# Weighted sums of two pairs together in slots 0 and 2 of an attention quad

## The reference

```python
attn = jnp.einsum('wqhd,wkhd->whqk', q * scale, k)
attn = attn + rel_bias[None]
attn = attn.reshape(B, nW, NH, N, N) + attn_mask[None, :, None]
attn = jax.nn.softmax(attn.reshape(B * nW, NH, N, N), axis=-1)
o = jnp.einsum('whqk,wkhd->wqhd', attn, v).reshape(B * nW, N, C)
o = o @ proj_w + proj_b
```

## Time and profile before

| | |
|---|---|
| median of 3 runs | 8522.53 us (8521.94 to 8527.99) |
| profiled execution | 8519.52 us, span of its instructions 8517.4 us |
| PE matmul busy | 7998.7 us, 94% of the span |
| PE weight loads | 5982.3 us, 70% |
| DVE, ACT, POOL busy | 72%, 60%, 63% |
| mean granted TensorE clock | 0.995 of full speed |

### The profile page before, as it was taken

One profiled execution on the slowest core, in us unless ns is written; L12 is line 12 of the kernel. 1 busy time (PEld: TensorE's weight loads), 2 busy tenths in 40 slices (PEclk: granted clock), 3 DMA queues, 4 the chain that ended last, 5 costly groups with the idle time before them and its releaser, 6 DMA issues.

```text
span 8517.4 us, 316110 instructions
## 1 busy us (share of the span) xinstructions
PE 7998.7 (94%) x111420; PEld 5982.3 (70%) x111420; DVE 6092.7 (72%) x18216; ACT 5147.7 (60%) x9120; POOL 5399.7 (63%) x6723
## 2 busy tenths in 40 slices
PE   3999999999999999999999999999999999999997
PEld 1777777777777777777767777777776677777766
DVE  4777767767776776776777677776686767777666
ACT  1755747646674664755767476574576647567456
POOL 6865646556785665655778465564677756556566
PEclk9999999999999999999999999999999999999998
DMA  2100010000011011000001101000100110000001
GB/s 42 22 13 10 15 27 15 10 12 13 10 21 31 13 20 22 15 6 16 9 15 21 27 16 27 15 15 4 20 4 19 24 22 15 7 13 14 6 19 23
DMA packets 596906, 142.14 MB, mean 17 GB/s; under 512 B 595660, under 2 KB 596256, under 8 KB 596471
## 3 DMA queue, kind: packets, MB, share of 16 engines
q1 hardware_dynamic: 574102, 131.41, 7.8%
q10 hardware_dynamic: 16865, 3.97, 0.3%
q0 software_dynamic: 5504, 1.21, 0.1%
HBM read 31.68 MB, written 19.27 MB: 6 GB/s over the span
## 4 chain that ended last, share of the span: by engine, by line
PE 71%; DVE 10%; issue 9%; ACT 3%; DVEq 2%; POOL 2%; ACTq 1%; POOLq 0%; DMA 0%
PE ps L876 12%; PE ps L932 11%; PE ps L838 8%; PE ps L864 7%; PE ps L948 7%; PE ps L977 7%; PE ps L883 5%; PE ps L901 4%; PE ps L911 3%; ACT PT L743 3%; DVE bst L995 2%; PE ps L819 2%; PE ps L920 2%; DVE xn L1114 2%; PE ps L962 2%
## 5 line engine op out<-in xcount | busy, mean ns | idle before, releaser
L618 POOL TENSOR_TENSOR S<-S,mx 113x588 f32<-113x588 f32 (+1 forms) x2048 | 2065.4, 1009 | 1543.8 <-DVE mx L1156 1539.4
L743 ACT ACTIVATE PT<-ps 98x588 f32<-98x588 f32 (+1 forms) x2048 | 1182.5, 577 | 1218.6 <-PE ps L932 1211.3
L1154 DVE TENSOR_TENSOR S<-ps,bias 113x588 f32<-113x588 f32 (+1 forms) x1536 | 963.4, 627 | 863.7 <-PE ps L864 863.7
L876 PEld LDWEIGHTS ps<-Vbd,PT 98*49 98x49 f32 x40960 | 1107.5, 125 | 658.6 <-issue 634.7
L876 PE MATMUL ps<-Vbd,PT 98*49 98x18 f32 (+1 forms) x40960 | 1321.4, 201 | 165.8 <-ACT PT L743 125.9
L1156 DVE TENSOR_REDUCE mx<-S 113x12 f32<-113x588 f32 (+1 forms) x2048 | 1359.6, 664 | 70.6
L932 PEld LDWEIGHTS ps<-ident,S 113*98 113x98 f32 x10240 | 1033.9, 128 | 477.6 <-issue 388.9
L932 PE MATMUL ps<-ident,S 113*98 113x113 f32 x10240 | 1338.7, 261 | 7.8 <-ACT S L725 4.6
L725 ACT ACTIVATE S<-S 113x588 f32<-113x588 f32 (+1 forms) x2048 | 1239.9, 605 | 63.1 <-POOL S L618 61.3
L948 PEld LDWEIGHTS ps<-w,G 128*98 128x98 f32 x12288 | 1149.8, 167 | 160.2 <-issue 86.3
L948 PE MATMUL ps<-w,G 128*98 128x96 f32 (+1 forms) x12288 | 1151.5, 250 | 2.7 <-DVE x L1221 2.4
(11 more groups left out here) (104 smaller groups left out, 10891.0 us busy)
## 6 DMA issues: line engine op xcount, KB each, us to landing
Vbd<-Vd SPq DMA_DIRECT2D x1536, 41.3 KB
Vbd<-Vd SPq DMA_DIRECT2D x512, 38.3 KB
mask<-L_conv_mask_matrix_dram SPq DMA_DIRECT2D x256, 37.5 KB
x<-x_dram SPq DMA_DIRECT2D x48, 84.0 KB
out_dram<-x SPq DMA_DIRECT2D x48, 84.0 KB
x<-x_dram SPq DMA_DIRECT2D x228, 10.5 KB
out_dram<-x SPq DMA_DIRECT2D x228, 10.5 KB
out_dram<-x SPq DMA_DIRECT2D x180, 18.4 KB
```

The costliest lines, as they stand in the source:

```text
L618: pool.tensor_tensor(v, v, m, ALU.subtract).then_inc(a_sub, 1)
L743: act.activation(PT[:, (s + 3) % 4, 0:blocks, :, :].rearrange("p (b t) w n -> p b (t w) n", b=banks), PTps[:, PT_BANK[l] - 3:PT_BANK[l] - ...
L876: last = pe.matmul(Ops[ROW2 * w:ROW2 * w + N, p, b, :].rearrange("p (a n) -> p a n", a=2), PT[:, p, b, w, :], v, start=True, stop=True)
L1154: dve.tensor_tensor(dst, scores, b, ALU.add).then_inc(a_bi, 1)
```

## The change

In PE's `attend` the weighted sums no longer stand in every slot. Slot 0 makes those of pairs 0 and 1 of quad i - 1, slot 2 those of pairs 2 and 3. The wait for a_o (now of quad i - 2) and for the spread of v stands at slot 0. Pairs 0 and 2 are thus summed one slot later than before (from slot 3 to slot 0, from slot 1 to slot 2), pairs 1 and 3 in the slots they had. The signal a_pv follows the sums of pair 3 in slot 2, as before. The number and shape of the matmuls are the same, and nothing changes on other engines.

```diff
--- before.py
+++ after.py
@@ -863,18 +863,20 @@
                                             keys, out = Kfull[rows, t, s, N * w:N * (w + 1)], Sps4[to, k, :]
                                         last = pe.matmul(out, q, keys, start=True, stop=True)
                                 last.then_inc(a_sc, 1)
-                            if on(-1) if s < 3 else on(0):
-                                wait(a_pte, i.pair(s - 3))
-                                p = (s + 1) % 4
-                                if s == 3:
-                                    wait(a_o, i - 1)
-                                    spread = (g * LAYER_QUADS + l * NQ + i.index - t + 2) * 32
-                                    pe.wait_ge(s_vb[t], spread if i.static else pe.snap(spread))
-                                for b in range(blocks):
-                                    for w in range(2):
-                                        v = values_of(Vbd[:, o if s < 3 else t, p, w, :, :], nh, b)
-                                        last = pe.matmul(Ops[ROW2 * w:ROW2 * w + N, p, b, :].rearrange("p (a n) -> p a n", a=2),
-                                                         PT[:, p, b, w, :], v, start=True, stop=True)
+                            if s in (0, 2) and on(-1):
+                                wait(a_pte, i.pair(s - 4))
+                                if s == 0:
+                                    wait(a_o, i - 2)
+                                    spread = (g * LAYER_QUADS + l * NQ + i.index - 1 - o + 2) * 32
+                                    pe.wait_ge(s_vb[o], spread if i.static else pe.snap(spread))
+                                for p in (s, s + 1):
+                                    if p % 2:
+                                        wait(a_pte, i.pair(p - 4))
+                                    for b in range(blocks):
+                                        for w in range(2):
+                                            v = values_of(Vbd[:, o, p, w, :, :], nh, b)
+                                            last = pe.matmul(Ops[ROW2 * w:ROW2 * w + N, p, b, :].rearrange("p (a n) -> p a n", a=2),
+                                                             PT[:, p, b, w, :], v, start=True, stop=True)
                                 if s == 2:
                                     last.then_inc(a_pv, 1)
                             if s == 0 and on(-2):
```

## The result

The changed kernel took 9004.47 us in the median of four runs (8949.17 to 9110.12), the kernel before 8523.15 us (8521.94 to 8527.99). The ratio is 1.054, 95% interval 1.0518 to 1.0563. I had forecast slower, 8791 us, in a range up to 8895: the direction was right and the size was not.

A forecast was written before the change was run, and what follows sets the result against it. It took slot 1 as bound by ACT's loop, slot 3 by the Ot stall then that loop, slots 0 and 2 by PE. Terms 70 + 207 - 8 = +269 us on 8519.5, plus 3 to the median: 8791 us, range 8725 to 8895.

The forecast's parts named there:

- Slot 1 is bound by copy of PT, copy of keys and exp on ACT: 12-head layers, slot 1: ACT's loop takes 2.65 us over PE's 2.50 us of work, so removing sums gains 0.
- T(3) to T(0): T(u) is the start of the transposes of S for pair u; this step, slot 1, was forecast unchanged at 2.65 us.
- The second pair of a double group: Slots 0 and 2, 12-head layers: a moved pair adds 0.55 us, or 0.66 us at the other end.
- The stall before the sums: Slot 3: PE's wait of about 0.3 us a quad for Ot (a_o) before pair 0's sums disappears.
- 11.46 + 0.81: Layers 1 and 2: a quad of 11.46 us before, plus 2 x 0.55 - 0.29 = +0.81 us for the change.
- 8519.5 + 70 + 207 + 3: Profiled execution before, plus layer 0's 70, layers 1 and 2's 207, and 3 us from that execution to the median.
- The rival in which PE alone decides: Whole kernel: PE's gap before the sums goes and nothing is paid, about 8359 us, or 8275; chance 6%.
- the one in which only slot 1 is held: Rival: exp does not hold slot 3, which falls to 1.95 us instead of 2.65; no change, 8522 us; chance 4%.
- -0.06 us a quad: Layer 3: net between -0.12 and 0 us a quad, transposes of Ot starting 0.32 us earlier; -8 us over 128 quads.
- the idle time would appear: Slots 1 and 3: PE idles some 0.7 us each before the transposes of S, put down to exp.
- My terms were 70, 207 and -8: Added us per run: layer 0 128 x 0.55, layers 1 and 2 256 x 0.81, layer 3 128 x -0.06.
- a larger price for a pair: Slots 0 and 2: 0.66 us a moved pair instead of 0.55, with layer 3 at 0, gives 8883 us.

The follow-up runs named there:

- layers 0 to 2 alone: The change made in layers 0 to 2 only, layer 3 as in the kernel before; against the kernel before: 8801.66 us, ratio 1.0319.
- layer 3 alone: The change made in layer 3 only, layers 0 to 2 as in the kernel before; against the kernel before: 8765.49 us, ratio 1.0297.
- the same move: Only pair 2's sums moved, slot 1 to 2: 8600.79 us; with keys moved too 8523.24; with keys and DVE's statistics moved 8393.17; kernel before 8523.15.
- the keys moved: The changed kernel with ACT's first and fourth copies of keys moved to slots 0 and 2, layer 3's one to slot 0: 8990.58 us, ratio 1.057.
- half A: Only pair 0's sums moved, slot 3 to slot 0; pair 2's as in the kernel before: 8895.35 us, ratio 1.0429 against the kernel before.

## Why the prediction came out too low

**What held.** Slot 1 is bound by copy of PT, copy of keys and exp on ACT: T(3) to T(0) stayed at 2.64 us, and fell to 2.17 when the copy of keys left the loop. The second pair of a double group costs 0.55 us, not 0.66. The stall before the sums vanished, and slot 3 fell to 2.64 us behind exp. Layers 1 and 2 came to 12.28 us a quad, where 11.46 + 0.81 = 12.27 was forecast. The run of layers 0 to 2 alone gives 8788 to 8791 us at full clock, against 8519.5 + 70 + 207 + 3 = 8800 by my sum. The rival in which PE alone decides and the one in which only slot 1 is held are both out.

**The term that was mis-sized: layer 3.** I took -0.06 us a quad, with the reason that the transposes of Ot could start as soon as Ot was ready, 0.32 us earlier. They also wait for a_vd, since they overwrite the bank that Vd is copied from. The trace of before could have told me, in the round of the earlier trace rows:

```profile
2010.64 0.55 DVE L1178 COPY Vd<-ps 98x384 f32<-98x384 f32 x1
...
2011.34 0.59 PE L911 MATMUL ps<-ident,Ot 113*96 113x113 f32 x4
```

The copy ends at 2011.19, 0.15 us before the transposes, so the sums that stood there covered that wait; without them it is bare. In the round shown above T(3) to T(2) takes 5.57 us (1967.32 to 1972.89), as before (5.58), and not 5.26 to 5.39, while T(2) to T(3) rose by the forecast 0.20 to 2.54 us (1964.78 to 1967.32). A quad took 8.16 us at full clock and not 7.9, +0.20 on the 7.96 of before, or 26 us in 128 quads instead of -8; the stages of layer 3 that kept the clock in the run of layer 3 alone, 262.2 us against 254.5, say 31.

**The term that was missing: the clock.** The sum assumed a full clock throughout. I had written that the idle time would appear, and had not asked what idle PE does to the clock. Of the four runs the time at half clock can be taken out, as an estimate: it is twice (1 - clock) times the span, less the 94 us that the kernel before has too (2 x 8517 x 0.0055, since its executions show 0.994 and 0.995), and of it a share of (12.64 - 8.16)/12.64 = 0.354 is lost.

| span, us | clock | at half clock beyond before, us | lost, us | rest, us |
|---|---|---|---|---|
| 8947.0 | 0.974 | 371 | 131 | 8816 |
| 8972.0 | 0.970 | 444 | 157 | 8815 |
| 9032.6 | 0.961 | 610 | 216 | 8817 |
| 9108.0 | 0.950 | 817 | 289 | 8819 |

The rest is the same within 4 us, so the spread of the runs is the clock's; the spans alone give 161 us for 446 us at half clock, a factor of 0.361. The factor 0.354 is that of layer 3, and some half-clock time lies elsewhere. The lengths of the stages at full clock lead to the same place without it. From the first to the last transposes of S, layer 0 takes 389.9 us against 372.1, layers 1 and 2 389.7 against 365.4, layer 3 262.2 against 254.5: four groups give 71 + 194 + 31 = 296 us, 8816 in all. My terms were 70, 207 and -8. So at full clock the change costs about 290 us, and 8816 lies inside my range; the loss through the clock, 130 to 290 us a run, takes it out.

The high end of the forecast, 8883, was built from a larger price for a pair, which was the wrong thing to doubt.

What stays open: why the gap of 0.8 to 0.9 us in layer 3 is enough and the two gaps of layers 0 to 2, up to 0.57 us in a round of 12.3, nearly never are, and what sets when in a stage the clock falls. The length of the gap by itself hardly decides it: half A idles 0.79 us in nearly every round of 11.8 us in layer 0 and kept the clock there. In the changed kernel's profile it fell 78 to 178 us into the four stages of layer 3, in that of half A 45 us into each of them. Why exp is followed sooner by the transposes when extra matmuls precede them is open too.

## What to carry to other kernels

When a change leaves the busiest engine's work as it is and moves it between slots, find for each slot the loop that closes over the other engines; work that moves out of a slot held by such a loop gains nothing, and where it arrives it costs its full time. Then look at what the emptied slot waits for, since every wait that the moved work covered is bare, and price the idle time on TensorE twice: once as time, once as clock. Open the loops first and then move the work: the same move cost 77 us before, nothing that could be told with one loop open, and saved 72 with both.

## What the runs showed of the hardware

- TensorE's clock fell from 2.4 to 1.2 GHz in steady work, with PE idle for 0.8 to 0.9 us in each round of 8.1 us, and no longer stop in between. The kernel before, which stops there for 0.44 us at the sums and for 0.51 us at most in the steady part of layer 3, kept it.
- Once at 1.2 GHz it stayed there for up to 270 us (362 with the keys moved), though PE then had hardly any gap (49.77 of 50 us busy). In all four stages of layer 3 of the changed kernel's profile it came back 8 to 9 us before the last transposes of S. The Trainium skill, "TensorE: Matmul & The Clock Gate", Part 1: The HAM clock gate, has the clock return after sustained activity; the rows of layer 3 don't show that here, while the first stretch in layer 0, 257 to 329 us, did end inside its stage, 270 us before the stage's last transposes of S.
- Two short matmuls that compute nothing, in that gap in each round, kept it at 2.4 GHz: 8670 us instead of 8895 for half A, mean clock 0.994 instead of 0.924 to 0.976.
- Two groups of small matmuls of the same tiling, one behind the other, cost 0.11 us less than two groups apart, 1.21 us for 48 matmuls against 2 x 0.66. That agrees with the drain at a change of tiling mode in the Trainium skill, "TensorEngine Tiling (Array Packing)", Key Properties; no run shows that the drain is what takes the 0.11 us.
